# Key block diagonals written by the eviction with a 0/1 column, and a packed layout for the small inputs

## The chip, the cores and the metric
The kernel runs on one core of a Trainium2 chip. The metric is the device time of one execution in microseconds (us); lower is better. The core has a matrix engine (PE), a vector engine (DVE), a scalar engine (ACT), a third elementwise engine (POOL) and a queue engine (SP) that issues nearly all DMAs. The engines run at the same time, each takes its own instructions strictly in order, and they wait for each other through semaphores.

## The reference, cut to what matters
Sixteen independent batch elements of 128 tokens by 256 channels, all float32, go through two blocks:

```python
m = silu(cond) @ w_ada + b_ada           # 9 vectors of 256 per batch element: shift, scale, gate, three times
h = ln(x) * (1 + sc_msa) + sh_msa        # SELF:  16 heads of 16, 128x128 scores per head
x = x + (softmax(q k^T / 4) v @ w_so + b_so) * g_msa
h = ln(x) * (1 + sc_mca) + sh_mca        # CROSS: keys and values from ctx, the 16 largest scores of 128 kept
x = x + (softmax(top16(q k^T / 4)) v @ w_co + b_co) * g_mca
h = ln(x) * (1 + sc_mlp) + sh_mlp        # MLP:   silu(a) * b of 1024 each
x = x + (silu(a) * b @ w_m2 + b_m2) * g_mlp
xq, xkv = ada_ln(x, cond), ada_ln(ctx, cond)   # LAST:  keys and values from the normalised ctx (CTX)
x = x + softmax(q k^T / 4) v @ Wp + bp
```

## The kernel before
Each batch element b runs through five stages: SELF, CTX (keys and values of both cross attentions, made from ctx), CROSS, MLP and LAST. Several batch elements are in flight, each in another stage.

**The order of the work** is fixed ahead of time. Five tables (SP_PLAN, POOL_PLAN, ACT_PLAN, DVE_PLAN, PE_PLAN, lines 52 to 133) give each step an offset, START gives each stage of each b a number, and steps() (L136) sorts by the sum. The numbers are sort keys and no times. A step stands in the order of its engine wherever the sum puts it, and if it has to wait, all that stands behind it on that engine waits too.

**Scores.** The scores of one attention of one b ("scores", L904 to 923) are eight matmuls into s_bank, four PSUM banks that hold all 16 heads. There is one s_bank, so the 48 score steps of the program take turns. Scores of SELF b and CROSS b are two turns or more apart, and the turn goes in the steady part LAST, CROSS, SELF. The next scores can start once the exponentials (and, for CROSS, the first cut of the top-16 search) have read the bank. All other matmul results go through a ring of four PSUM banks, taken in the order of use and given back by their eviction.

Two heads share one score matmul: 32 rows of q hold two heads of 16, and the keys come as a block diagonal, head 0's rows in the left 128 columns with zeros on the right, head 1's rows in the right 128 columns with zeros on the left. Keys are in k_self, k_cross and k_last with 2, 2 and 4 slots for batch elements.

**How the block diagonals are made before.** "qk" (L872) projects q and k of SELF for b into one ring bank. DVE evicts all of it with its bias into qk_t (L687, 128x512). "k2" (L885) does the same for the keys of CROSS and LAST into k2_t (L694, 128x512). POOL has set the block tiles to zero at the start (L465). Then SP, at "place" (L425 to 436), waits for the eviction and issues eight DMAs per tile that copy 16 rows each to their half (L373): eight for SELF, sixteen for CROSS and LAST, 24 for each b. Scores wait for k_placed (L910), and evictions of k2 wait until the DMAs have read k2_t (L692).

**ctx.** It is loaded once as 128 tokens by 256 (L361). "turn" of CTX (L860 to 871) transposes it raw (two matmuls against the identity, L867) and normalised (two more, L870); ACT copies the raw half out (L535).

**Setup before.** cond comes as 16x256, goes through tanh on ACT and two DVE operations, is transposed by PE (L829) and copied. Thirteen bias vectors come by twelve small DMAs (L386) as 60 rows of 128, are transposed by PE (L824) and spread by DVE (L616 to 633). The gates' biases come by four DMAs (L390, L392). "mods" (L842) multiplies silu(cond) with the weights that give scale and shift of a stage, "rows" (L851) gives the gates, which go to DRAM and come back as broadcast loads (L364). The three parts of w_ada come as 768 KB each.

Of the kernel before, what the change touches and what calls it, by code (L numbers as in the profile page):

```python
# [51 lines left out]
SP_PLAN = (
    ("load", "cond", None, 226.752), ("load", "gb", None, 235.686), ("load", "so", None, 248.240),
    ("load", "rows", None, 254.344), ("load", "ada0", None, 263.081), ("place", SELF, SELF, 298.546),
    ("load", "ada2", None, 303.744), ("load", "co", None, 311.157), ("load", "x0", None, 312.291),
    ("load", "ada1", None, 317.622), ("load", "qkv", None, 320.311), ("load", "ctx0", None, 320.321),
    ("load", "x1", None, 330.262), ("load", "bp", None, 331.814), ("place", CROSS, CROSS, 346.351),
    ("load", "ss_kv", None, 358.160), ("load_gates", SELF, SELF, 367.495), ("load", "lkv", None, 369.922),
    ("load_ctx", 0, CTX, 370.194), ("store_rows", MLP, None, 397.858), ("load", "x2", None, 411.296),
    ("load", "kv", None, 422.952), ("first_gates", MLP, None, 424.059), ("store_rows", CROSS, None, 427.406),  # L60
    ("store_rows", SELF, None, 433.778), ("load", "x6", None, 434.351), ("load", "lp", None, 436.552),
    ("first_gates", SELF, None, 444.342), ("load", "ctx1", None, 447.588), ("load_gates", CROSS, CROSS, 449.495),
    ("load", "ss_q", None, 456.751), ("store_y", 0, LAST, 465.795), ("load_gates", MLP, MLP, 468.644),
    ("load", "q", None, 468.660), ("load", "x4", None, 480.238), ("load", "x3", None, 485.938),
    ("load_x", 0, LAST, 488.314), ("load", "lq", None, 493.225), ("first_gates", CROSS, None, 493.235),
    ("load", "m1", None, 510.757), ("load", "x5", None, 529.760), ("load", "m2", None, 531.567),
)
# [10 lines left out]
ACT_PLAN = (
    ("shift", SELF, SELF, -36.227), ("v", 0, SELF, -2.370), ("shift", CTX, CTX, 6.791),
    ("exp", (SELF, 0), SELF, 7.093), ("exp", (SELF, 1), SELF, 8.413), ("exp", (SELF, 2), SELF, 9.622),  # L80
    ("exp", (SELF, 3), SELF, 9.942), ("v2", 0, CTX, 26.683), ("T", (SELF, 0), SELF, 33.733),
    ("T", (SELF, 1), SELF, 34.298), ("T", (SELF, 2), SELF, 34.531), ("T", (SELF, 3), SELF, 36.876),
    ("inv", SELF, SELF, 37.653), ("shift", CROSS, CROSS, 52.002), ("exp", (CROSS, 0), CROSS, 66.004),
    ("exp", (CROSS, 1), CROSS, 73.999), ("exp", (CROSS, 2), CROSS, 74.922), ("exp", (CROSS, 3), CROSS, 78.653),
    ("top_exp", 0, CROSS, 81.146), ("T", (CROSS, 0), CROSS, 81.913), ("T", (CROSS, 1), CROSS, 81.920),
    ("T", (CROSS, 2), CROSS, 82.806), ("T", (CROSS, 3), CROSS, 83.460), ("inv", CROSS, CROSS, 84.882),
    ("shift", MLP, MLP, 91.150), ("tanh", 0, MLP, 97.308), ("tanh", 1, MLP, 98.175), ("half", 0, MLP, 103.625),
    ("half", 1, MLP, 105.370), ("shift", LAST, LAST, 125.349), ("exp", (LAST, 0), LAST, 131.955),
    ("exp", (LAST, 1), LAST, 133.173), ("exp", (LAST, 2), LAST, 133.815), ("exp", (LAST, 3), LAST, 136.413),
    ("T", (LAST, 0), LAST, 139.376), ("T", (LAST, 1), LAST, 142.428), ("T", (LAST, 2), LAST, 145.168),  # L90
    ("T", (LAST, 3), LAST, 146.105), ("inv", LAST, LAST, 150.744),
)
DVE_PLAN = (
    ("stats", SELF, SELF, -62.647), ("aggr", SELF, SELF, -61.830), ("cond", 0, None, -60.987),
    ("stats", CTX, CTX, -25.918), ("qk", 0, SELF, -24.776), ("aggr", CTX, CTX, -22.218),
    ("max", (SELF, 0), SELF, 1.754), ("bias", 0, None, 2.756), ("silu", 0, None, 6.770),
    ("max", (SELF, 1), SELF, 7.259), ("k2", 0, CTX, 15.767), ("inv", SELF, SELF, 20.340), ("o", SELF, SELF, 39.280),
    ("rows", SELF, None, 39.486), ("gate", SELF, SELF, 43.321), ("add", SELF, SELF, 43.495),
    ("stats", CROSS, CROSS, 43.948), ("aggr", CROSS, CROSS, 45.523), ("q", CROSS, CROSS, 61.535),
    ("rows", MLP, None, 63.287), ("mods", SELF, None, 64.135), ("top_a", 0, CROSS, 65.492),  # L100
    ("top_a", 1, CROSS, 65.498), ("cut_a", 0, CROSS, 65.723), ("cut_a", 1, CROSS, 65.845),
    ("top_a", 2, CROSS, 66.141), ("top_b", 0, CROSS, 67.290), ("top_b", 1, CROSS, 67.343),
# [908 lines left out]
```

## Time and profile before

| what | value |
|---|---|
| three runs | 689.52 us median, 685.43 to 690.34 |
| profiled execution | 688.72 us |
| its span | 686.5 us (2.2 us lie outside) |
| mean granted clock of PE over the span | 0.963 |
| PE, DVE, ACT, POOL busy in us | 615.2, 522.9, 496.2, 372.8 |

A busy share tells how long an engine had an instruction in it. PE's matmuls are pipelined, so its busy time is not all work at full rate. Cover each other: what an engine does while another one is the late one costs nothing. The granted clock is in tenths or as a fraction of full speed, 2.4 GHz; half of it is 1.2 GHz.

### The profile page before, as it was taken

The numbers are of one execution on the slowest core, as the hardware profiler recorded it, in microseconds if no ns is written. First come the engines' busy times: TensorE is split into PE (matmuls) and PEld (weight loads), VectorE is DVE, ScalarE is ACT, GpSimd is POOL, SyncE is SP. The second block draws the span as 40 slices with busy tenths as digits, with TensorE's granted clock in tenths as the row PEclk, the third lists the DMA queues.
The fourth block names the chain that finished last, engine by engine and source line by source line (L and its number), as shares of the span: only waits on it lengthen the run. The fifth ranks groups of instructions, "written<-read, shape, count | busy, mean of one in ns | idle before, by whom it ended". The sixth has DMA issues, their size and how long they took to land.

```text
span 686.5 us, 18283 instructions
## 1 busy us (share of the span) xinstructions
PE 615.2 (90%) x5899; PEld 534.3 (78%) x5899; DVE 522.9 (76%) x2201; ACT 496.2 (72%) x1906; POOL 372.8 (54%) x623
## 2 busy tenths in 40 slices
PE   3966787899999999999999999999999999886786
PEld 1755576798989788888889898989897988775564
DVE  3223857889898979798979898898989797968232
ACT  0154464888888787979887887878888878755174
POOL 3223543757575747665756666674747472737220
PEclk9898899999999999999999999999999999999697
DMA  6352261110203020202020202102020201010000
GB/s 210 117 169 74 65 216 25 40 24 17 76 8 88 6 81 14 84 12 79 16 77 19 75 21 66 29 23 73 12 74 5 80 9 45 11 40 1 24 1 16
DMA packets 37740, 36.43 MB, mean 53 GB/s; under 512 B 8115, under 2 KB 29151, under 8 KB 37391
## 3 DMA queue, kind: packets, MB, share of 16 engines
q1 hardware_dynamic: 37647, 35.27, 16.9%
q8 instruction: 48, 0.79, 0.5%
q14 instruction: 45, 0.37, 0.2%
HBM read 26.75 MB, written 2.20 MB: 42 GB/s over the span
## 4 chain that ended last, share of the span: by engine, by line
DVE 42%; PE 25%; ACT 15%; POOL 6%; issue 5%; SPq 4%; DMA 2%; POOLq 0%; DVEq 0%
ACT probs L566 13%; DVE left L724 9%; DVE left L737 9%; DVE top L713 7%; DVE top L731 7%; PE ring L816 6%; PE ring L810 5%; PE s_bank L920 4%; DVE neg_max L705 3%; SPq L373 3%; PE ring L976 3%; DVE mlp L784 2%; POOL left L505 2%; PE ring L933 2%; PE ring L953 2%
## 5 line engine op out<-in xcount | busy, mean ns | idle before, releaser
L566 ACT ACTIVATE probs<-s_bank,neg_max 128x128 f32<-128x128 f32 x512 | 181.1, 411 | 14.0 <-DVE neg_max L705 12.6
L976 PE MATMUL ring<-h_t,w_m 128*128 128x128 f32 x1024 | 126.4, 280 | 5.2 <-DVE k_t L694 3.5
L566 ACT ACTIVATION_READ_ACCUMULATOR probs<-s_bank,neg_max 128x1 f32 x512 | 129.0, 252 | 0.0
L976 PEld LDWEIGHTS ring<-h_t,w_m 128*128 128x128 f32 x1024 | 120.6, 195 | 10.7 <-issue 8.3
L573 ACT ACTIVATE probs_t<-ring 128x512 f32<-128x512 f32 x192 | 110.6, 629 | 23.7 <-PE ring L933 23.1
L563 ACT ACTIVATE probs<-s_bank,neg_max 128x128 f32<-128x128 f32 x256 | 73.7, 399 | 49.3 <-DVE left L724 49.3
L705 DVE TENSOR_REDUCE neg_max<-s_bank 128x8 f32<-128x1024 f32 x64 | 76.1, 1203 | 25.5 <-PE s_bank L920 25.1
L538 ACT ACTIVATE h_t<-ring,mod_all 128x128 f32<-128x128 f32 x160 | 63.2, 482 | 40.9 <-PE ring L870 40.8
L505 POOL TENSOR_TENSOR left<-left,probs 128x512 f32<-128x512 f32 x64 | 83.6, 1306 | 9.8 <-POOL left L501 0.4
L519 POOL TENSOR_TENSOR mlp<-mlp 128x512 f32<-128x512 f32 x32 | 40.8, 1274 | 72.1 <-ACT mlp L595 72.1
L933 PE MATMUL ring<-ident,probs 128*128 128x128 f32 x512 | 71.8, 275 | 6.6 <-ACT probs L566 3.2
L478 POOL TENSOR_SCALAR ln_var<-ln_mv 128x1 f32<-128x1 f32 x80 | 15.4, 193 | 110.0 <-DVE ln_mv L682 108.2
L933 PEld LDWEIGHTS ring<-ident,probs 128*128 128x128 f32 x512 | 59.9, 142 | 11.6 <-ACT probs L566 6.1
L724 DVE MATCH_REPLACE8 left<-top,s_bank 128x128 f32<-128x128 f32 x256 | 68.7, 277 | 0.0
L737 DVE MATCH_REPLACE8 left<-top,left 128x128 f32<-128x128 f32 x256 | 67.5, 273 | 0.0
L984 PE MATMUL ring<-w_m,mlp 128*128 128x256 f32 x256 | 58.2, 380 | 2.6 <-POOL mlp L519 2.5
L713 DVE MAX8 top<-s_bank 128x8 f32<-128x128 f32 x256 | 54.8, 279 | 2.5 <-PE s_bank L920 2.4
L984 PEld LDWEIGHTS ring<-w_m,mlp 128*128 128x128 f32 x256 | 47.4, 190 | 9.1 <-POOL mlp L519 3.3
L595 ACT ACTIVATE mlp<-ring,bias_cols 128x128 f32<-128x128 f32 x128 | 36.8, 381 | 24.2 <-PE ring L976 23.9
L731 DVE MAX8 top<-left 128x8 f32<-128x128 f32 x256 | 53.7, 276 | 0.6
L501 POOL TENSOR_SCALAR left<-left 128x512 f32<-128x512 f32 x64 | 39.6, 618 | 25.8 <-DVE left L737 22.9
L497 POOL TENSOR_TENSOR x_res<-x_res,gates 128x256 f32<-128x256 f32 x48 | 34.9, 728 | 33.9 <-DMA gates<-rows_dram 33.7
(127 smaller groups left out, 1270.1 us busy)
## 6 DMA issues: line engine op xcount, KB each, us to landing
gates<-rows_dram SPq DMA_DIRECT2D x48, 256.0 KB, 4.0
x_res<-in_x SPq DMA_DIRECT2D x16, 128.0 KB, 3.8
ctx_in<-in_ctx SPq DMA_DIRECT2D x16, 128.0 KB, 3.9
k_self<-qk_t SPq DMA_DIRECT2D x128, 16.0 KB, 2.3
k_cross<-k_t SPq DMA_DIRECT2D x128, 16.0 KB, 1.9
k_last<-k_t SPq DMA_DIRECT2D x128, 16.0 KB, 1.9
w_m<-in_L_xcond_w_m SPq DMA_DIRECT2D x1, 2048.0 KB, 7.7
out_y<-x_res SPq DMA_DIRECT2D x16, 128.0 KB, 1.7
```

Source lines behind the costliest of these rows:

```text
L505: nc.gpsimd.tensor_tensor(left[:, u], left[:, u], probs[:, CROSS, u], ALU.add).then_inc(masked, 1)
L563: e = nc.scalar.activation(probs[:, k, u, j], s_bank[:, u, P * j:P * j + P], ACT.Exp, bias=neg_max[:, k, n:n + 1])
L566: e = nc.scalar.activation(probs[:, k, u, j], s_bank[:, u, P * j:P * j + P], ACT.Exp, bias=neg_max[:, k, n:n + 1], accum_out=row_sum[:, k, ...
L573: nc.scalar.activation(dst, bank("T", which, b)[:], ACT.Relu if k == CROSS else ACT.Copy).then_inc(pt_ready, 1)
L705: nc.vector.tensor_reduce(neg_max[:, k, 8 * half:8 * half + 8], s_bank[:, 2 * half:2 * half + 2].rearrange("p u (j t) -> p (u j) t", t=P), ...
L713: e = nc.vector.max(top16[:, 4 * u + j, 0:8], s_bank[:, u, P * j:P * j + P])
L724: e = nc.vector.match_replace(left[:, u, j], top16[:, 4 * u + j, 0:8], s_bank[:, u, P * j:P * j + P], GONE)
L731: e = nc.vector.max(top16[:, 4 * u + j, 8:16], left[:, u, j])
L737: e = nc.vector.match_replace(left[:, u, j], top16[:, 4 * u + j, 8:16], left[:, u, j], GONE)
L933: e = nc.tensor.transpose(d[:, P * j:P * j + P], src[:, j], ident[:])
L976: e = nc.tensor.matmul(d[:, P * j:P * j + P], w_m1[:, c, at:at + P], h_t[:, MLP, c], start=(c == 0), stop=(c == CK - 1))
L984: e = nc.tensor.matmul(d[:, 0:C], glu[:, j // 4, j % 4], w_m2[:, j], start=(j == 0), stop=(j == HB - 1))
```

## The change
The key blocks are written by the eviction itself. A column `halves` (128x2) holds 0 or 1 per row: column 0 is 1 on rows of head 0 of each pair, column 1 on rows of head 1. POOL sets up its source once (three small instructions) and DVE makes the two columns (two small instructions). key_blocks() then issues for each 128 channels one scalar_tensor_tensor from PSUM: (k + bias) * halves, 256 elements wide, the PSUM operand read twice. That is two instructions for SELF and four for CROSS and LAST per b. q of SELF has its own eviction, 256 wide. All `place` steps, the k_placed semaphores and the zeroing of the key tiles go. "k2" now waits for the scores that read the slot it writes.

The host lays out inputs differently (reordering only): weights with 128 partitions outermost and contiguous rows, cond transposed as 128x32, all bias columns as 128x54, the gates' biases in one array, and a second copy of ctx that is already transposed (ctx_t). So the transposes of ctx (L867), its copy out (L535), and the transposes of cond and biases go. w_ada's parts come split in scale/shift (512 KB) and gate (256 KB), w_qkv in q/k (512 KB) and v (256 KB). A second load per b brings ctx_t (128 KB). The next ctx_in load waits for "norm" instead of "turn". The five tables and START are written anew, so the order of steps changes in many places; the order of the 48 score steps among themselves is the same as before.

```diff
-    SELF: (123.491, 159.058, 201.581, 240.471, 280.069, 319.014, 357.908, 396.794,
+    SELF: (189.635, 227.561, 267.927, 306.804, 346.245, 385.716, 425.902, 465.078,
 ...
-    ("load", "rows", None, 254.344), ("load", "ada0", None, 263.081), ("place", SELF, SELF, 298.546),
+    ("load", "cond", None, -835.363), ("load", "ada0", None, -819.429), ("load", "vecs", None, -732.506),
 ...
-            def place(kind, b, src):
-                s = b % SLOTS[kind]
-                if b >= SLOTS[kind]:
-                    sp.wait_ge(scores_done, PE_N["scores", kind, b - SLOTS[kind]])
-                for g in range(8):
-                    rows_g = slice(16 * g, 16 * g + 16)
-                    sp.dma_start(k_blocks[kind][rows_g, s, :, g % 2, :], src[rows_g]).then_inc(k_placed[kind, s], 16)
 ...
                 if name == "load_ctx" and b + 2 < B:
-                    sp.wait_ge(turned, PE_N["turn", CTX, b])
+                    sp.wait_ge(normed, POOL_N["norm", CTX, b])
                     load_ctx(b + 2)
+                if name == "load_ctx_t" and b + 2 < B:
+                    sp.wait_ge(k2_done, b + 1)
+                    sp.wait_ge(v2_done, b + 1)
+                    load_ctx_t(b + 2)
 ...
-                    if k == CTX:
-                        nc.scalar.copy(ctx_t[:].rearrange("p c t -> p (c t)"), src[:, 0:C])
-                        at = C
 ...
+            def key_blocks(k, b, d, at):
+                for c in range(CK):
+                    src = d[:, C + at + P * c:C + at + P * c + P]
+                    e = nc.vector.scalar_tensor_tensor(
+                        out=k_blocks[k][:, b % SLOTS[k], c], in0=src.unsqueeze(1).broadcast_to([P, 2, P]),
+                        scalar=bias_cols[:, NK + 2 * k + c:NK + 2 * k + c + 1],
+                        in1=halves[:].unsqueeze(2).broadcast_to([P, 2, P]), op0=ALU.add, op1=ALU.mult)
+                return e
 ...
                 if name == "qk":
-                    if b >= 2:
-                        dve.wait_ge(k_placed[SELF, b % 2], 16 * 8 * (b // 2))
+                    if b >= SLOTS[SELF]:
+                        dve.wait_ge(scores_done, PE_N["scores", SELF, b - SLOTS[SELF]])
                     dve.wait_ge(qk_done, b + 1)
-                    nc.vector.tensor_tensor(qk_t[:, b % 2], blocks(bank("qk", 0, b), 4), cols(NQ_SELF, 4),
-                                            ALU.add).then_inc(qk_ready, 1)
+                    d = bank("qk", 0, b)
+                    nc.vector.tensor_tensor(q_t[:, SELF, b % 2], blocks(d, CK), cols(NQ + 2 * SELF, CK), ALU.add)
+                    key_blocks(SELF, b, d, 0).then_inc(qk_ready, 1)
                 if name == "k2":
-                    if b:
-                        for k in (CROSS, LAST):
-                            dve.wait_ge(k_placed[k, (b - 1) % SLOTS[k]], 16 * 8 * ((b - 1) // SLOTS[k] + 1))
+                    for k in (CROSS, LAST):
+                        if b >= SLOTS[k]:
+                            dve.wait_ge(scores_done, PE_N["scores", k, b - SLOTS[k]])
                     dve.wait_ge(k2_done, b + 1)
-                    nc.vector.tensor_tensor(k2_t[:], blocks(bank("k2", 0, b), 4), cols(NK_CTX, 4),
-                                            ALU.add).then_inc(k2_ready, 1)
+                    d = bank("k2", 0, b)
+                    key_blocks(CROSS, b, d, -C)
+                    key_blocks(LAST, b, d, 0).then_inc(k2_ready, 1)
```

**How the order moves.** The rows below give the line, the instruction and, in brackets, the semaphores it waits for. First PE from the program's start, before. probs_t holds w_ada's part for SELF, mlp those for MLP and CROSS, probs the weights of scale and shift of CTX (later of LAST):

```order
L829 MATMUL ring<-ident,probs_t 128x16 [waits setup_dve,consts_ready]
...
L824 MATMUL ring<-ident,probs_t 128x60 [waits rows_loaded]
L816 MATMUL ring<-probs_t,silu_t 16x256 [waits bias_ready,silu_ready,w_loaded_so,w_loaded_ada0]
...
L816 MATMUL ring<-w_so,bv_rows 16x256 x2
L816 MATMUL ring<-mlp,silu_t 16x256 [waits silu_ready,bias_ready,w_loaded_ada2]
...
L842 MATMUL ring<-silu_t,probs_t 128x16 [waits silu_ready,w_loaded_ada0]
...
L842 MATMUL ring<-silu_t,mlp 128x16 [waits bias_evicted,w_loaded_ada2,silu_ready]
...
L842 MATMUL ring<-silu_t,mlp 128x16 [waits rows_evicted,w_loaded_ada1,silu_ready]
```

The same stretch of PE in the changed kernel:

```order
L812 MATMUL ring<-silu_t,probs_t 128x16 [waits w_loaded_ada0,silu_ready,consts_ready]
...
L796 MATMUL ring<-probs_t,silu_t 16x256 [waits bias_ready,silu_ready,w_loaded_so,w_loaded_ada0g]
...
L796 MATMUL ring<-w_so,bv_rows 16x256 x2
L835 MATMUL ring<-ident,x_norm 128x128 [waits normed]
...
L812 MATMUL ring<-silu_t,probs 128x16 [waits w_loaded_ss_kv,silu_ready]
...
L790 MATMUL ring<-h_t,w_qkv 128x128 [waits h_ready,mods_ready,w_scaled,w_loaded_qk]
...
L796 MATMUL ring<-w_qkv,h_t 128x256 [waits rows_evicted,h_ready,w_loaded_v]
```

The transposes of cond and biases are gone, "mods" of SELF is first, and "mods" of MLP and CROSS and "rows" of MLP have moved behind the first "qk".

SP around the first two placements, before:

```order
L420 DMA rows_dram<-left 16x512 [waits rows_ready]
L358 DMA x_res<-in_x 128x256
L373 DMA k_self<-qk_t 16x2x128 [waits zeroed,qk_ready]
L373 DMA k_self<-qk_t 16x2x128 x7
L355 DMA w_kv<-in_L_xcond_w_kv 128x2x512
L364 DMA gates<-rows_dram 128x512 [waits rows_stored3]
...
L361 DMA ctx_in<-in_ctx 128x256
L373 DMA k_self<-qk_t 16x2x128 [waits qk_ready]
...
L355 DMA w_q<-in_L_xcond_w_q 128x2x256
L373 DMA k_cross<-k_t 16x2x128 [waits zeroed,k2_ready]
```

SP from its first waiting instruction on in the changed kernel:

```order
L399 DMA rows_dram<-left 16x512 [waits rows_ready]
L358 DMA x_res<-in_x 128x256
L355 DMA l_q<-in_w_lq 128x512
...
L355 DMA mlp<-in_w_ada 128x2x512
L364 DMA ctx_t<-in_ctx_t 128x256
...
L367 DMA gates<-rows_dram 128x512 [waits rows_stored0]
...
L355 DMA w_q<-in_w_q 128x512
L364 DMA ctx_t<-in_ctx_t 128x256 [waits v2_done,k2_done]
...
L361 DMA ctx_in<-in_ctx 128x256 [waits normed]
L355 DMA w_m<-in_w_m 128x4096
```

No placement stands between the loads any more, and 21 DMAs are issued ahead of the first wait.

DVE in one turn of the steady part, from the eviction of q and k of SELF to the top-16 search, before:

```order
L687 TENSOR_TENSOR qk_t<-ring,bias_cols 128x512
L677 BN_STATS ln_stats<-x_res 128x6
L705 TENSOR_REDUCE neg_max<-s_bank 128x8
...
L677 BN_STATS ln_stats<-ctx_in 128x6
...
L779 TENSOR_TENSOR mlp<-ring,bias_cols 128x512
...
L694 TENSOR_TENSOR k_t<-ring,bias_cols 128x512
...
L699 TENSOR_TENSOR q_t<-ring,bias_cols 128x256
L748 RECIPROCAL inv_row<-row_sum 128x4x2x2
L784 SCALAR_TENSOR_TENSOR mlp<-mlp 128x512 x2
L713 MAX top<-s_bank 128x8 x8
```

The same in the changed kernel:

```order
L666 TENSOR_TENSOR q_t<-ring,bias_cols 128x256
L587 SCALAR_TENSOR_TENSOR k_self<-ring,bias_cols,halves 128x256 x2
L685 TENSOR_REDUCE neg_max<-s_bank 128x8 x2
L655 BN_STATS ln_stats<-ctx_in 128x6
...
L587 SCALAR_TENSOR_TENSOR k_cross<-ring,bias_cols,halves 128x256 x2
L587 SCALAR_TENSOR_TENSOR k_last<-ring,bias_cols,halves 128x256 x2
L759 TENSOR_TENSOR mlp<-ring,bias_cols 128x512 x2
L728 RECIPROCAL inv_row<-row_sum 128x4x2x2
L679 TENSOR_TENSOR q_t<-ring,bias_cols 128x256
L764 SCALAR_TENSOR_TENSOR mlp<-mlp 128x512 x2
L693 MAX top<-s_bank 128x8 x8
```

The keys' evictions stand at the same places, are longer, and k2's now stands ahead of both linear evictions of the MLP (the step "lin").

## Rows read from the trace of the kernel before

**Rows 1.** Windows: length, busy (instructions) by engine, clock, DMA share, GB/s.

```profile
0.00:20.00 20.00, 8.82 (x39) 4.97 (x39) 8.04 (x20) 1.70 (x2) 8.23 (x15) 1.00 0.63 216
20.00:40.00 20.00, 15.94 (x98) 12.37 (x98) 4.22 (x11) 2.86 (x8) 2.89 (x8) 0.78 0.30 104
172.59:208.18 35.59, 35.40 (x364) 31.75 (x363) 31.57 (x137) 30.74 (x120) 22.71 (x39) 1.00 0.16 46
244.63:282.00 37.37, 35.59 (x364) 31.78 (x363) 31.40 (x137) 31.03 (x120) 23.19 (x39) 1.00 0.15 46
354.20:390.55 36.35, 35.49 (x364) 31.81 (x363) 31.98 (x137) 30.75 (x120) 22.54 (x39) 1.00 0.16 48
```

**Rows 2.** Timeline of PE, score steps: start, length, instruction, [idle before <-releaser].

```profile
37.57 1.67 PE L920 MATMUL s_bank<-k_self,qk_t 32*128 32x256 f32 x16 [4.06 <-DMA k_self<-qk_t]
51.86 2.09 PE L920 MATMUL s_bank<-k_self,qk_t 32*128 32x256 f32 x16 [1.01 <-issue]
68.55 2.09 PE L920 MATMUL s_bank<-k_cross,q_t 32*128 32x256 f32 x16 [4.84 <-DVE q_t L699]
108.95 1.51 PE L920 MATMUL s_bank<-k_cross,q_t 32*128 32x256 f32 x16
137.02 1.15 PE L920 MATMUL s_bank<-k_last,q_t 32*128 32x256 f32 x16 [0.16 <-ACT probs L566]
571.41 1.15 PE L920 MATMUL s_bank<-k_last,q_t 32*128 32x256 f32 x16 [1.07 <-ACT probs L566]
```

**Rows 3.** Timeline of PE in the first 35 us.

```profile
11.90 1.89 PE L816 MATMUL ring<-probs_t,silu_t 128*16 128x256 f32 x4 [3.19 <-DMA probs_t<-in_L_xcond_w_ada]
17.13 2.16 PE L842 MATMUL ring<-silu_t,probs_t 128*128 128x16 f32 x16
19.14 5.31 PE L842 MATMUL ring<-silu_t,mlp 128*128 128x16 f32 x32
28.15 2.05 PE L810 MATMUL ring<-h_t,w_qkv 128*128 128x128 f32 x16
32.91 0.38 PE L867 MATMUL ring<-ident,ctx_in 128*128 128x128 f32 x2
```

**Rows 4.** DMA issues: queue, count, size of one, median us to landing.

```profile
probs_t<-in_L_xcond_w_ada SPq DMA_DIRECT2D x1, 768.0 KB, 4.5
probs<-in_L_xcond_Wss_kv SPq DMA_DIRECT2D x1, 512.0 KB, 10.6
k_self<-qk_t SPq DMA_DIRECT2D x128, 16.0 KB, 2.3
```

**Rows 5.** Timeline of SP, issues of the placements and one load.

```profile
45.45 5.05 SPq L373 DMA_DIRECT2D k_self<-qk_t  x8
53.06 5.46 SPq L373 DMA_DIRECT2D k_cross<-k_t  x8
64.03 0.83 SPq L358 DMA_DIRECT2D x_res<-in_x  x2
97.08 5.18 SPq L373 DMA_DIRECT2D k_self<-qk_t  x8
```

**Rows 6.** Timeline of DVE.

```profile
66.90 0.43 DVE L677 BATCH_NORM_STATS2 ln_stats<-x_res 128x6 f32<-128x256 f32 x1 [4.89 <-DMA x_res<-in_x]
104.61 0.43 DVE L677 BATCH_NORM_STATS2 ln_stats<-ctx_in 128x6 f32<-128x256 f32 x1 [6.94 <-DMA ctx_in<-in_ctx]
353.65 0.42 DVE L699 TENSOR_TENSOR q_t<-ring,bias_cols 128x256 f32<-128x256 f32 x1 [0.81 <-PE ring L810]
353.99 0.68 DVE L687 TENSOR_TENSOR qk_t<-ring,bias_cols 128x512 f32<-128x512 f32 x1
354.59 0.42 DVE L677 BATCH_NORM_STATS2 ln_stats<-x_res 128x6 f32<-128x256 f32 x1
361.11 0.69 DVE L779 TENSOR_TENSOR mlp<-ring,bias_cols 128x512 f32<-128x512 f32 x1 [0.43 <-PE ring L976]
362.91 1.49 DVE L784 SCALAR_TENSOR_TENSOR mlp<-mlp 128x512 f32<-128x512 f32 x2 [0.26 <-ACT mlp L587]
```

More of the change, by code:

```diff
@@ L57 @@
[L57 to L61, printed above, removed]
@@ L77 @@
+    ("scale", LAST, None, 324.348),
 )
 ACT_PLAN = (
[L79 to L83, printed above, removed]
@@ L92 @@
 )
 DVE_PLAN = (
[L94 to L102, printed above, removed]
-    ("cut_b", 0, CROSS, 67.535), ("cut_a", 2, CROSS, 68.629), ("mods", MLP, None, 68.704),
-    ("cut_b", 1, CROSS, 68.737), ("top_b", 2, CROSS, 68.910), ("top_a", 3, CROSS, 69.295),
@@ new lines @@
+    ("silu_mul", 0, MLP, 110.337), ("silu_mul", 1, MLP, 110.928), ("gate", MLP, MLP, 121.630),
+    ("add", MLP, MLP, 123.598), ("stats", LAST, LAST, 125.556), ("aggr", LAST, LAST, 126.459),
+    ("q", LAST, LAST, 136.983), ("max", (LAST, 0), LAST, 140.295), ("max", (LAST, 1), LAST, 140.863),
+    ("inv", LAST, LAST, 148.846), ("o", LAST, LAST, 161.791), ("mods", CTX, None, 165.205),
+    ("rows", SELF, None, 166.782), ("add", LAST, LAST, 168.553), ("rows", CROSS, None, 183.314),
+    ("rows", MLP, None, 200.055), ("mods", MLP, None, 245.611), ("mods", CROSS, None, 246.801),
@@ L115 @@
+    ("mods", LAST, None, 260.307), ("last", 0, None, 310.092),
 )
 PE_PLAN = (
-    ("silu", 0, None, -313.698), ("bias", 0, None, -226.294), ("rows", SELF, None, -212.684),
-    ("turn", SELF, SELF, -43.063), ("qk", 0, SELF, -30.856), ("rows", MLP, None, -13.780), ("v", 0, SELF, -8.038),
-    ("scores", SELF, SELF, -2.255), ("turn", CTX, CTX, 4.022), ("k2", 0, CTX, 11.855), ("v2", 0, CTX, 20.806),
-    ("mods", SELF, None, 24.708), ("T", (SELF, 0), SELF, 27.657), ("T", (SELF, 1), SELF, 28.424),
@@ L133 @@
+    ("scores", LAST, LAST, 131.855), ("T", (LAST, 0), LAST, 138.341), ("T", (LAST, 1), LAST, 139.915),
+    ("T", (LAST, 2), LAST, 143.901), ("T", (LAST, 3), LAST, 146.327), ("inv", LAST, LAST, 147.533),
+    ("sums", LAST, LAST, 152.412), ("out", LAST, LAST, 161.343), ("mods", CTX, None, 162.231),
+    ("rows", CROSS, None, 181.589), ("rows", MLP, None, 199.664), ("mods", CROSS, None, 238.898),
+    ("mods", MLP, None, 240.469), ("mods", LAST, None, 241.796), ("last", 0, None, 305.966),
 )
@@ L141, in steps @@
         yield name, which, b
-BANKED = {"bias", "silu", "mods", "rows", "last", "turn", "qk", "v", "k2", "v2", "q", "T", "inv", "sums", "out", "up", "down"}
+BANKED = {"mods", "rows", "last", "turn", "qk", "v", "k2", "v2", "q", "T", "inv", "sums", "out", "up", "down"}
 USE = {}
```

353 lines of the change are left out of this document (174 added, 179 removed).

## The prediction, made before the result was known
> **What bounds the kernel now.** I read the page's busy times first (PE 615 of 686.5 us, DVE 523), then the start times of the score steps, because they cut the program into a fill, a steady part and a tail. The first scores of SELF start at 37.57, the first of LAST at 137.02 and the thirteenth of LAST at 571.41 [rows 2]. So the fill is 137.0 us, twelve turns take 434.4 us, which is 36.2 each, and the tail is 686.5 - 571.4 = 115.1.
>
> Then the windows. In a steady turn of 35.59 to 37.37 us PE is busy 35.4 to 35.6 at full clock, DVE 31.4 to 32.0, ACT 30.7 to 31.0 [rows 1]. PE has almost no gap, so the steady part is PE's own work plus 0.2 to 1.8 us per turn. The fill is another matter: in the first 20 us PE is busy 8.8, and from 20 to 40 its clock is 0.78, a mix of 2.4 and 1.2 GHz [rows 1]. There the timeline shows what it waits for. The first scores wait 4.06 us for the placement of k_self [rows 2]. Eight placement issues hold SP for 5.0 to 5.5 us and the last lands 2.3 us after its issue [rows 4, 5]; in that time no load behind them is issued. Two such loads come late: x_res is issued at 64.03, behind 16 placements, and DVE stands 4.89 us for it, which keeps q of CROSS from PE's first CROSS scores for 4.84 us; and ctx_in, behind the placements from 97.08 to 102.26, holds DVE for 6.94 us in front of k2's eviction [rows 2, 5, 6].
>
> **The change, part by part**
>
> *Until the first scores.* Before, PE starts its main work at 11.90, when 768 KB of w_ada have come: a load of 4.5 us that was issued after 18 others [rows 3, 4]. In the changed kernel 512 KB of it are SP's second DMA. It is issued near 1.2 and, by that row, lands by 5.2. From there I add what stands in PE's order up to the first scores: "mods" of SELF 2.2, "rows" of SELF 1.9 + 1.9, a turn and the shift on ACT 1.8, "mods" of CTX 2.2, "qk" 2.05, "v" 1.7, "rows" of CROSS 1.9 + 1.9, two turns 0.7, all at the durations of the slow clock [rows 3]. That is 18.3, so the first scores come at 23.5, which is **-14.1**. Of this, 5.31 (the two "mods" for MLP and CROSS) and 1.9 ("rows" of MLP) are only moved behind the scores [rows 3] and come back below. The loads could be later than I take them: 512 KB for CTX took 10.6 us from issue to landing in a full queue [rows 4], and issued near 5 that would be 15.6 instead of the 12.8 at which PE asks for it. Bounds: -8 (weights late by 3, the moved work at once in the way) to -17 (no wait and a warm clock).
>
> The Trainium skill (DMA: Bandwidth & Descriptors, Specifications) wants at least 512 bytes per transfer for full rate, and cond (128 bytes a row) and the bias columns (216 bytes a row) now lie under that, where before they lay at or above it. By that page these two loads are poor. They are 16 and 27 KB, and the rows here do not show such a load. Nothing in the sum rests on this.
>
> *First to second scores of SELF, 14.3 us before.* The second placement is issued from 45.45 to 50.50, and the scores start at 51.86 [rows 2, 5]. It goes; "rows" of MLP, a longer "qk" and "v2" now lie in the same stretch. **-1**, bounds -4 to +2.
>
> *Second scores of SELF to the first of CROSS, 16.7 us.* The 4.84 us go, since the x loads are now ahead of any late wait on SP; 5.31 at a cold clock, about half at a warm one, for the moved "mods" come in, partly where PE would wait for SELF's residual anyway. **-1.5**, bounds -5 to +2.
>
> *First to second scores of CROSS, 40.4 us.* DVE's 6.94 go with the placements ahead of ctx_in. PE had other work for a part of it, so I take **-4.9**, the same size as the other stall; bounds -3 to -7. From there to the first LAST scores (28.1 us) I take nothing. The fill gives -14.1 - 1 - 1.5 - 4.9 = **-21.5**; LAST's first scores come at 115.5. Bounds together -11 to -29.
>
> *DVE in the steady part.* Its instructions overlap, so I take start-to-start times: 0.34 for 256 wide (353.65 to 353.99) and 0.60 for 512 (353.99 to 354.59) [rows 6]. The trace has no scalar_tensor_tensor from PSUM; the one from SBUF of 512 takes 1.49 for two, much like the other forms, so I take 0.34 for 256. SELF's keys: 3 x 0.34 instead of 0.60, +0.42. k2: 4 x 0.34 instead of 0.60, +0.76. Together **+1.18 per batch element**, DVE 31.5 + 1.2 = 32.7 of 36. It stays under PE. What hides it: SELF's eviction stands before LAST's maxima, which wait for PE's scores; k2's stands between these maxima and silu_mul, while ACT makes LAST's exponentials. "lin" of the second half starts at 361.11 only because PE is that late (0.43 idle), and silu_mul again waits 0.26 for ACT at 362.91 [rows 6]. With k2's 0.76 and the second stats ahead of "lin", I count on lin starting at most as late as PE's second "up" allows. I charge 0; if that cover were gone, all of it would be 1.18 x 12 = +14 over the steady part.
>
> The Trainium skill (VectorE: DVE Perf Modes, the section on the TRN2 errata) puts an operation from PSUM at 120 cycles plus its elements, at 0.96 GHz: 0.39 us for 256 wide and 0.66 for 512. By it the change adds 7 x 0.39 - 2 x 0.66 = 1.4 us per element, against the 1.18 of the rows; the rows decide.
>
> *PE.* Two raw transposes of ctx per element go, 0.22 us of work (two take 0.38 with overlap, 0.11 start to start) [rows 3]. They stand just ahead of LAST's scores, in the stretch that is PE's own. -0.22 per turn.
>
> *ACT* loses one copy per element, *SP* 24 issues and gains one. Neither was late in the steady part, except where SP's placements delayed ctx_in: the turn of 37.37 against 35.59 is the size of it [rows 1]. On the other hand the new order lets POOL's last mask wait at other places. I take **-0.2 per turn, -2.4** over twelve. Bounds: -0.8 (all turns as short as the best one less 0.22, 35.4) to +1.18, so -10 to +14.
>
> *Tail.* After the last k2 nothing of the change is in it but the order; 0, bounds -2 to +2.
>
> **Sum:** 688.7 (profiled execution) - 21.5 - 2.4 = 664.8. The median of the runs is 0.8 above that execution, so 665.
>
> **The rivals**
>
> *Weights or gates come late in the fill.* For: the first 20 us already move 216 GB/s at 0.63 of the DMA engines' time [rows 1], and the changed kernel asks for ss_kv, qk, v and co within 18 us. Against: 21 DMAs go out without a wait. The fill then gives -11, and the time is 689.5 - 11 - 2.4 = 676.
>
> *DVE's extra work is not covered.* For: DVE is at 88% of a turn and the top-16 search is one long DVE stretch on which SELF's scores wait. Against: the new evictions do not stand in that stretch. +14 on the steady part: 689.5 - 21.5 + 14 = 682 at the full 1.18, 679 with PE's 0.22 and the ctx waits taken off.
>
> *The steady part drops to PE's floor.* With no placement, no late ctx_in and fewer transposes, turns of 35.4: 689.5 - 21.5 - 10 = 658.
>
> *Slower: k2's eviction delays the MLP.* It now stands ahead of both "lin". If (k + bias) * halves, with its PSUM operand read twice, took much longer than a plain eviction, "lin" would be late, then tanh on ACT, silu_mul, and with them the start of the top-16 search, which sets SELF's scores and so the turn. To eat 23.9 us over about 14 turns it needs 1.7 per turn on the path. The cover there is about 0.7 (0.43 + 0.26 [rows 6]), and the six instructions take the place of 1.20 - 0.34 = 0.86 (two plain evictions less q's own), so together they would have to cost 0.86 + 0.7 + 1.7 = 3.26, which is 0.54 us each from start to start. At 0.60, the pace of a 512 wide one [rows 6], the turn grows by 6 x 0.60 - 0.86 - 0.7 = 2.0 and the time is 689.5 - 21.5 + 14 x 2.0 = 696. Against: the output has 256 elements per instruction, and 256 wide ones take 0.42 here whatever their kind.
>
> **How the numbers follow.** Forecast (650 to 672) 0.52; late weights (676) 0.17; uncovered DVE work (679 to 682) 0.12; PE's floor (658 and under) 0.14; slower by k2 0.05. The predicted time is **665**. The range takes in the floor with a better fill, 689.5 - 29 - 8 = 652, and the uncovered DVE work, 682. About 1% (7 us) is what a measurement of this kernel tells from no change, its three runs spread over 0.7%. Faster by over 1% (under 682.6): 0.91; within 1%: 0.05 (uncovered work together with late weights); slower: 0.04.
>
> **What would show it.** In the trace after: "mods" of SELF on PE by 6, first scores of SELF at 21 to 27, first of LAST at 110 to 122; key_blocks instructions of about 0.42 us with 0.34 between starts; DVE busy 32 to 33.5 per turn; turns of 35.5 to 36.5. It would be wrong if the fill still ended past 128, if turns were 37 and more with DVE named as what PE waits for, or if PE waited for weights between 5 and 20 us for more than 5 us in sum.

## The result, and the profile after

The changed kernel takes 683.43 us (median of 20 runs, 680.40 to 689.52) against 689.41 for the kernel before (20 runs, 685.43 to 691.55). The ratio is 0.9933, with a 95% interval of 0.9912 to 0.9954. That is 0.7% faster where 665 us was forecast, outside the range of 652 to 682. The profiled execution took 683.1 us with a span of 681.4 (before: 688.72 and 686.5).

The score steps cut its time into the same three parts as before. The start times on PE, to be held against [rows 2]:

```profile
22.95 1.15 PE L887 MATMUL s_bank<-k_self,q_t 32*128 32x256 f32 x16
33.81 1.15 PE L887 MATMUL s_bank<-k_self,q_t 32*128 32x256 f32 x16
50.07 1.15 PE L887 MATMUL s_bank<-k_cross,q_t 32*128 32x256 f32 x16
84.01 1.15 PE L887 MATMUL s_bank<-k_cross,q_t 32*128 32x256 f32 x16
113.38 1.15 PE L887 MATMUL s_bank<-k_last,q_t 32*128 32x256 f32 x16
566.78 1.15 PE L887 MATMUL s_bank<-k_last,q_t 32*128 32x256 f32 x16 [0.59 <-ACT probs L542]
```

The fill ends at 113.38 instead of 137.02: -23.6 us. The twelve turns behind it take 566.78 - 113.38 = 453.4 us, 37.78 each, where they took 434.4, 36.20 each: **+19.0**. The tail is 114.6 against 115.1. So the fill gained what was forecast, and four fifths of it were lost again, evenly over the steady turns. The windows of four turns, in the columns of [rows 1], show it:

```profile
151.33:188.07 36.74, 36.12 (x361) 31.36 (x360) 34.06 (x142) 30.59 (x119) 22.75 (x39) 1.00 0.13 37
188.07:225.88 37.81, 36.23 (x362) 31.41 (x361) 34.52 (x142) 30.59 (x119) 22.59 (x39) 1.00 0.14 37
264.03:301.98 37.95, 36.23 (x362) 31.41 (x361) 34.91 (x142) 30.45 (x119) 22.76 (x38) 1.00 0.08 28
301.98:339.68 37.70, 36.23 (x362) 31.42 (x361) 34.50 (x142) 30.58 (x119) 23.16 (x39) 1.00 0.11 35
```

The clock is full in all of them, so it is no part of the loss. DVE is busy about 3 us more per turn, where seven evictions of 256 (six of keys, one of q) instead of two plain ones of 512 should give 1.2 to 1.5. The surplus is found in the chain of waits, the view that says which piece of work each next one waited for. One turn of the kernel before, from scores to scores (start, length, what; the middle of the top-16 search left out):

```profile
327.01 1.29 DVE mlp L784 x2
328.30 1.60 DVE top L713 x8
329.90 0.06 DVE neg_max L721
...
331.03 0.07 DVE neg_max L721
...
335.54 0.07 DVE neg_max L721
...
340.32 0.07 DVE neg_max L721
...
343.62 0.63 POOL left L501
```

The same stretch in the changed kernel:

```profile
272.75 2.01 DVE mlp L764 x2
274.76 1.60 DVE top L693 x8
276.36 0.06 DVE neg_max L701
...
279.05 0.06 DVE neg_max L701
...
281.22 1.13 DVE neg_max L701
...
287.83 0.31 DVE neg_max L701
...
291.37 0.63 POOL left L479
```

From the end of silu_mul (the line "mlp") to the mask of GpSimd (POOL) on which the next transposes wait, it is 16.61 us after (274.76 to 291.37) and 15.32 before (328.30 to 343.62). All 1.29 of it is in one tiny operation, neg_max<-top: a tensor_scalar that negates four numbers per partition, in the step cut_a. silu_mul itself takes 2.01 instead of 1.29. From scores to scores these two turns last 35.90 and 37.95 us, and the 1.29 and the 0.72 of silu_mul are 2.01 of the 2.05 between them. The sums over the execution (busy time, mean ns of one), before first:

```profile
L784 DVE SCALAR_TENSOR_TENSOR mlp<-mlp 128x512 f32<-128x512 f32 x32 | 21.6, 709 | 3.6 <-ACT mlp L587 3.6
L721 DVE TENSOR_SCALAR neg_max<-top 128x4 f32<-128x4 f32 x64 | 12.5, 196 | 0.0
```

```profile
L764 DVE SCALAR_TENSOR_TENSOR mlp<-mlp 128x512 f32<-128x512 f32 x32 | 27.5, 893 | 3.9 <-ACT mlp L563 3.9
L701 DVE TENSOR_SCALAR neg_max<-top 128x4 f32<-128x4 f32 x64 | 29.1, 455 | 0.0
```

And this is what stands beside them on POOL in that turn of the changed kernel:

```profile
272.75 2.01 DVE L764 SCALAR_TENSOR_TENSOR mlp<-mlp 128x512 f32<-128x512 f32 x2 [0.27 <-ACT mlp L563]
273.05 1.16 POOL L475 TENSOR_TENSOR x_res<-x_res,b_last 128x256 f32<-128x256 f32 x1
274.17 1.86 POOL L475 TENSOR_TENSOR x_res<-x_res,gates 128x256 f32<-128x256 f32 x2
...
279.83 2.50 POOL L497 TENSOR_TENSOR mlp<-mlp 128x512 f32<-128x512 f32 x2 [3.46 <-ACT mlp L571]
281.14 1.21 DVE L701 TENSOR_SCALAR neg_max<-top 128x4 f32<-128x4 f32 x1
```

The two glu multiplies of POOL run from 279.83 to 282.33. neg_max starts at 281.14 and ends at 282.35, with the second of them. The last neg_max of the search, the 0.31 of the chain, ends with another POOL operation, a product for the masks that runs to 288.12:

```profile
286.85 1.27 POOL L483 TENSOR_TENSOR left<-left,probs 128x512 f32<-128x512 f32 x1
...
287.76 0.39 DVE L701 TENSOR_SCALAR neg_max<-top 128x4 f32<-128x4 f32 x1
```

In the kernel before, the two multiplies start 2.22 us apart in the turn of the chain above and 2.68 in the next one, and the same neg_max lands behind the second. In this next turn it meets a residual add that runs to 371.92, and takes 0.39:

```profile
367.28 1.28 POOL L519 TENSOR_TENSOR mlp<-mlp 128x512 f32<-128x512 f32 x1 [4.02 <-ACT mlp L595]
...
369.96 1.28 POOL L519 TENSOR_TENSOR mlp<-mlp 128x512 f32<-128x512 f32 x1 [1.40 <-ACT mlp L595]
...
371.20 0.72 POOL L497 TENSOR_TENSOR x_res<-x_res,gates 128x256 f32<-128x256 f32 x1
...
371.57 0.39 DVE L721 TENSOR_SCALAR neg_max<-top 128x4 f32<-128x4 f32 x1
```

Over the whole trace of the changed kernel it is the same: 34 of the 64 neg_max start while a POOL operation has more than 0.1 us to go, and each of them ends 0.02 to 0.03 us after that operation. The other 30 take 0.139 to 0.151 us. Of the time above 0.15 us, 13.8 us stand beside the glu multiplies, 4.1 beside the mask products, 1.9 beside adds and copies.

The tables of the change did this: ACT's two "half" steps now follow each other directly, so POOL's glu multiplies do too, and the third cut_a stands one place earlier in DVE's top-16 order (seven steps ahead of it, before eight). The second of these is tested below; ACT's part was not put back by itself.

**Theory A:** DVE operations of some forms (neg_max, a tensor_scalar from SBUF to SBUF, and silu_mul with two inputs in SBUF) wait until the POOL operation in progress has ended. The new order brought neg_max (and silu_mul) into such collisions; the key evictions cost nothing. **Rival B:** the key evictions are the cost, since they lengthen DVE's work. **Rival C:** anything on DVE at that place is held up.

### The profile page after: what moved, and what is told of

Read it like the earlier page. It is cut to its first block, busy times and chain, and to the rows that moved or that the text cites. A ratio compares the mean times of both kernels' runs of the same rounds, so it can differ in the third digit from the quotient of the medians.

```text
span 681.4 us, 17865 instructions
## 1 busy us (share of the span) xinstructions
PE 617.0 (91%) x5864; PEld 529.8 (78%) x5864; DVE 562.6 (83%) x2276; ACT 493.0 (72%) x1891; POOL 367.8 (54%) x623
## 4 chain that ended last, share of the span: by engine, by line
DVE 44%; PE 31%; ACT 16%; POOL 5%; issue 2%; DMA 1%; SPq 1%; DVEq 0%; POOLq 0%; ACTq 0%
ACT probs L542 13%; DVE left L704 9%; DVE left L717 9%; PE ring L796 8%; PE ring L790 7%; DVE top L693 7%; DVE top L711 7%; DVE mlp L764 4%; DVE neg_max L701 3%; PE ring L920 3%; PE s_bank L887 3%; POOL left L483 3%; PE ring L900 3%; DVE neg_max L685 3%; PE ring L943 2%
## 5 line engine op out<-in xcount | busy, mean ns | idle before, releaser
L549 ACT ACTIVATE probs_t<-ring 128x512 f32<-128x512 f32 x192 | 112.2, 629 | 40.4 <-PE ring L900 40.2
L943 PE MATMUL ring<-h_t,w_m 128*128 128x128 f32 x1024 | 121.2, 277 | 1.8 <-ACT h_t L514 1.8
L943 PEld LDWEIGHTS ring<-h_t,w_m 128*128 128x128 f32 x1024 | 118.3, 194 | 2.3 <-ACT h_t L514 2.3
L514 ACT ACTIVATE h_t<-ring,mod_all 128x128 f32<-128x128 f32 x160 | 66.2, 509 | 38.9 <-PE ring L835 38.9
L951 PE MATMUL ring<-w_m,mlp 128*128 128x256 f32 x256 | 60.9, 392 | 2.3 <-POOL mlp L497 2.1
L900 PE MATMUL ring<-ident,left 128*128 128x128 f32 x256 | 38.2, 283 | 20.3 <-POOL left L483 14.9
L900 PEld LDWEIGHTS ring<-ident,left 128*128 128x128 f32 x256 | 28.0, 142 | 32.1 <-POOL left L483 18.9
```

What stands on the lines that cost most here:

```text
L549: nc.scalar.activation(dst, bank("T", which, b)[:], ACT.Relu if k == CROSS else ACT.Copy).then_inc(pt_ready, 1)
L900: e = nc.tensor.transpose(d[:, P * j:P * j + P], src[:, j], ident[:])
L943: e = nc.tensor.matmul(d[:, P * j:P * j + P], w_m1[:, c, at:at + P], h_t[:, MLP, c], start=(c == 0), stop=(c == CK - 1))
L951: e = nc.tensor.matmul(d[:, 0:C], glu[:, j // 4, j % 4], w_m2[:, j], start=(j == 0), stop=(j == HB - 1))
```

## The experiments

**neg_reduce.** One operation takes another form, in the changed kernel:

```
- nc.vector.tensor_scalar(neg_max[:, CROSS, 4*u:4*u+4].unsqueeze(2), top16[:, 4*u:4*u+4, 0:1], -1.0, None, ALU.mult)
+ nc.vector.tensor_reduce(neg_max[:, CROSS, 4*u:4*u+4], top16[:, 4*u:4*u+4, 0:1], AX.X, ALU.max, negate=True)
```

> The changed kernel, with the one small step neg_max<-top (128x4, two per quarter of the CROSS scores... four per batch, a tensor_scalar from SBUF to SBUF) written as a tensor_reduce with negate of the same four numbers. Theory A (that tensor_scalar is held up by GpSimd's two glu multiplies: 1.13 and 0.31 us of it stand in the chain of one turn, where the kernel before has 0.06 to 0.07 each): the op costs 0.05 to 0.15 us every time, a steady turn falls from 37.8 to 36.3 to 36.8 us, the whole to 662 to 670 us. Rival B (the four more key evictions on VectorE are what made the turn longer): the op gets shorter but the turn stays at 37.4 or more and the whole within 3 us of 683. Rival C (any op that reads SBUF there is held up): the reduce takes 1.2 us in the same place, no change.

Measured: 665.3 us, ratio 0.9647 (0.9610 to 0.9683), twelve turns of 36.45. Same numbers, same place, same neighbours on POOL, and the operation is free of the wait (36 of the 64 start with a POOL operation in progress, and none takes over 0.201 us):

```profile
L701 DVE TENSOR_REDUCE neg_max<-top 128x4 f32<-128x4 f32 x64 | 10.2, 159 | 0.0
```

In the same turn as above (now 36.65 us long, 37.95 before the edit) its four pieces of the chain are 0.06, 0.06, 0.07 and 0.06, and the search takes 15.29 us. All of the search's extra time is gone; silu_mul still takes 2.02. B and C fall. The same kernel once more:

> The first substitution once more, unchanged, beside the kernel before on the same chip, because its runs spread from 663 to 668 us: 662 to 669 us, turn 36.3 to 36.6.

Measured: 667.81 us, ratio 0.9685 (0.9647 to 0.9723), turns of 36.45 again. Of the 5.1 us between the two profiled executions (spans 661.0 and 666.1), 2.7 lie in the fill and 2.4 in the tail.

**before_neg_reduce.** The same edit in the kernel before.

> The same substitution in the kernel before. Theory A: there the op was mostly clear of the glu multiplies (mean 0.196 us of 64, 12.5 us in all), so at most 4 to 6 us come off, 683 to 688 us. Rival: if the reduce is a gain by itself, whatever stands beside it, then 10 us or more come off here as well (under 679).

Measured: 684.83 us, ratio 0.9924 (0.9897 to 0.9951), 36.03 a turn instead of 36.20. The form of the operation is worth 5 us where it rarely collides and 16 to 18, by the medians, where it collides in every turn.

**before_keys.** The kernel before, its tables and loads kept, with the key evictions alone:

```
- nc.vector.tensor_tensor(k2_t[:], blocks(bank("k2", 0, b), 4), cols(NK_CTX, 4), ALU.add)
+ key_blocks(CROSS, b, d, -C, NK_CTX)
+ key_blocks(LAST, b, d, 0, NK_CTX + CK)
- place(CROSS, b, k2_t[:, 0:CK]); place(LAST, b, k2_t[:, CK:2 * CK])      (and the same for SELF)
```

> The kernel before with the key blocks written by the eviction (no placements, no zeroing of key blocks, the odd/even columns set up), everything else, loads and the tables with the order of the work, as before. Theory A (the new order of the top-16 steps and of the glu steps costs the 1.6 us a turn, not the evictions): steady turn 36.0 to 36.6 us, and with the placements gone from the fill the whole at 670 to 680 us. Rival B (the evictions on VectorE cost it): turn at 37.2 or more, 685 to 700 us.

Measured: 671.72 us, ratio 0.9738 (0.9709 to 0.9767); fill 119.60, turns of 36.27. So the change from placements to evictions costs 0.07 us a turn and takes 17.4 us out of the fill, and this part of the change alone beats the whole of it by 11.7 us.

**neg_reduce_keys_twice.** neg_reduce with LAST's two key evictions written a second time, to a spare tile.

> The changed kernel with the tensor_reduce, and the two key evictions of LAST (2 x 0.40 to 0.48 us) written a second time, into a spare tile, in each of the 16 k2 steps: 0.8 to 0.9 us more of VectorE a turn. Theory A (the k2 evictions stand where VectorE waits anyway): 0 to 0.15 us a turn, 665 to 668 us in all. Rival B (they delay lin, tanh, silu_mul and so the top-16 steps, all of it uncovered): 0.85 x 16 = 13.6 us more, 677 to 680 us. Half covered: 671 to 673.

Measured: 663.96 us, ratio 0.9643 (0.9611 to 0.9676), turns of 36.51, +0.06. Even 0.8 us more of such work on DVE is covered.

**top_order.** The changed kernel with DVE's sixteen top-16 steps in the order of the kernel before (only due times in the table exchanged).

> The changed kernel with the 16 top-16 steps of VectorE put back into the order that they had in the kernel before (the second cut ahead of the third search, the third cut after the second late search), nothing else. Theory A: the third cut's neg_max op comes one step (about 0.5 to 0.9 us) later and lands mostly behind the two glu multiplies, so its wait falls from 1.2 us to 0.3 or less, and the turn to 36.8 to 37.3, the whole to 668 to 677 us. If the op runs into another GpSimd op instead, less comes off: 677 to 683 us. Rival B: 683, as the change.

Measured: 675.15 us, ratio 0.9788 (0.9756 to 0.9819), turns of 36.90; neg_max costs 17.4 us in all, mean 271 ns. The order of these sixteen steps alone was 0.9 of the 1.6 us a turn.

**glu_split.** Each glu multiply of POOL cut into four of 128x128; neg_max is a tensor_scalar as in the change.

```
+ for j in range(4):
+     nc.gpsimd.tensor_tensor(glu[:, half, j], tanh_a[:, half, j], glu[:, half, j], ALU.mult)
```

> The changed kernel with each of the two glu multiplies of GpSimd (128x512, 1.25 us) cut into four of 128x128; the tensor_scalar neg_max<-top stays. Theory A (a tensor_scalar of VectorE that reads and writes SBUF waits until the GpSimd operation that holds the port has ended, whatever its own size): its wait falls from up to 1.2 us to at most the length of a piece (0.3 to 0.5 us), the turn from 37.8 to 37.0 to 37.5 us, the whole to 671 to 680 us; GpSimd's extra instructions may give 0.3 of it back. Rival (it waits until GpSimd has no work left at all, or for something else than the multiplies): 1.2 us stays, 683 or more.

Measured: 673.62 us, ratio 0.9784 (0.9744 to 0.9823), turns of 37.21. Now neg_max waits for a piece, not for 1.2 us, although POOL works on for 1.6 us behind it. In 15 of the 16 batch elements it takes 0.415 to 0.429:

```profile
277.20 3.36 POOL L498 TENSOR_TENSOR mlp<-mlp 128x128 f32<-128x128 f32 x8 [3.47 <-ACT mlp L573]
278.50 0.42 DVE L703 TENSOR_SCALAR neg_max<-top 128x4 f32<-128x4 f32 x1
```

So the wait is set by the one POOL operation in progress. Beside the mask products, which were not cut, neg_max still takes up to 0.87 us, and the mean of all 64 is 336 ns.

**neg_reduce_top_order.** Both edits.

> Both at once: neg_max<-top as a tensor_reduce, and the top-16 steps in the order of the kernel before. Theory A: with the op immune, the order has nothing left to dodge, so the time is that of the first substitution, 665.3, within 2 us (663.5 to 667.5), turn 36.3 to 36.6. Rival: the order is worth something by itself (masks of GpSimd and transposes reached earlier): 2 to 6 us less, 659 to 663, or more.

Measured: turns of 36.44, as with the reduce alone (36.45), and a profiled execution of 662.63 us. The median is 669.8 (ratio 0.9728, 0.9691 to 0.9765), 2.3 above the expectation; its four other runs lie at 669 to 670. Their mean granted clock was 0.959 to 0.962, against 0.974 in the profiled one. That goes with the longer time, but no trace shows where those 7 us lie. On the steady turns theory A holds: with the operation immune, the order is worth nothing.

**neg_reduce_skip_late and neg_reduce_skip_gap.** These went for silu_mul. In the first, POOL's residual adds of LAST and SELF are due behind the glu multiplies; in the second, behind the spread and ahead of them.

> The changed kernel with the tensor_reduce, and GpSimd's residual adds (skip) of LAST and SELF moved from ahead of the glu multiplies to behind them, so that they no longer lie beside VectorE's silu_mul (two inputs in SBUF, 2.02 us for two in a turn where the kernel before takes 1.29 to 1.4). Theory A: silu_mul falls to 1.3 to 1.5 us, 0.4 to 0.7 us a turn, the whole to 655 to 661 us. Rival 1: the adds then delay the masks of the top-16 cut and with them the transposes, so it comes out at 665 or more. Rival 2: PE bounds the turn by then (36.2 busy of 36.4) and nothing is gained, 664 to 666.

> The changed kernel with the tensor_reduce, and GpSimd's residual adds of LAST and SELF moved into the 3.5 us in which GpSimd waits for ScalarE's half steps, ahead of the glu multiplies and behind the spread, so that only the MLP add may lie beside silu_mul, and the masks are not behind them. Theory A (silu_mul's two SBUF inputs are held up by the adds): silu_mul 1.3 to 1.5 us for two instead of 2.02, turn 35.9 to 36.2, the whole 657 to 662 us. Rival: the glu multiplies are late and the masks with them, or silu_mul is held up by the norm of GpSimd that takes the adds' place: no gain, 664 to 668.

Measured: 670.93 us (ratio 0.9764, 0.9701 to 0.9827), turns of 37.02; and 664.81 us (0.9663, 0.9622 to 0.9705), turns of 36.44. Both missed. The first made POOL's masks late: the transposes of the masked scores waited 16.2 us for them in all, 6.9 with neg_reduce_top_order. And silu_mul did not get shorter in either (867 and 922 ns), because POOL, which works down its list without a break, just ran its next operations there. In the second:

```profile
266.91 2.01 DVE L764 SCALAR_TENSOR_TENSOR mlp<-mlp 128x512 f32<-128x512 f32 x2 [0.26 <-ACT mlp L563]
267.22 1.16 POOL L475 TENSOR_TENSOR x_res<-x_res,gates 128x256 f32<-128x256 f32 x1
268.32 0.86 POOL L490 COPY inv_wide<-inv_row 128x256 f32<-128x256 f32 x1
```

The add that takes 0.73 us elsewhere takes 1.16 and the copy 0.86 instead of 0.40. Both engines lose here. Neither order tried kept POOL away; a wait did.

**neg_reduce_skip_hold.** The second of these, and the add of MLP waits for silu_mul:

```
+ if which == MLP:
+     pool.wait_ge(silu_done, DVE_N["silu_mul", 1, b])
```

> The kernel of the run before (tensor_reduce, the adds of LAST and SELF in GpSimd's gap), and GpSimd's add of MLP waits for the second silu_mul too, so that neither it nor the spread behind it lies beside silu_mul. Theory A (any GpSimd operation from and to SBUF that has started holds up silu_mul, there an add of 1.16 us and a copy of 0.86 us in the 2.01 us): silu_mul takes 1.29 to 1.35 us for two in every turn, 0.4 to 0.7 us less a turn on average where it was 2.01 (1.84 on average), so 0.3 to 0.6 a turn, 655 to 662 us. Rival: what comes off silu_mul is waited for elsewhere (GpSimd's glu multiplies and masks start later, or PE), and the turn stays at 36.3 or more, 663 to 668.

Measured: **655.65 us, ratio 0.9523 (0.9494 to 0.9553)**, turns of 35.99, the fastest of all. This kernel differs from neg_reduce_skip_gap by the wait alone, so the wait is worth 0.45 us a turn. The adds are back at their own length. silu_mul takes 1.29 to 1.31 us for two in six of the twelve steady turns and 1.47 to 1.49 in the other six, so the expected 1.29 to 1.35 in every turn was only half met; in the turn of 263.99 the norm's last POOL operation (263.77 to 264.32) is still in progress when it starts. POOL's wait costs nothing, since POOL idled later for ACT's "half" anyway (3.44 us before glu, now 2.46):

```profile
L766 DVE SCALAR_TENSOR_TENSOR mlp<-mlp 128x512 f32<-128x512 f32 x32 | 22.0, 722 | 3.9 <-ACT mlp L565 3.9
L477 POOL TENSOR_TENSOR x_res<-x_res,gates 128x256 f32<-128x256 f32 x48 | 34.8, 726 | 38.7 <-DVE mlp L766 38.7
```

## Why the prediction was wrong, and where it was right

*Until the first scores, -14.1.* Measured -14.6 (37.57 to 22.95). "mods" of SELF starts at 5.12, forecast 5.2, and weights are waited for only once more, 1.47 us, for ss_kv. That the rest came out is partly luck. All steps were taken "at the durations of the slow clock", and "mods" of SELF (3.57 us against 2.2) and "qk" (3.66 against 2.05) took longer, by 2.7 from start to start, while "v" (1.05 against 1.7) and "rows" of CROSS (1.04 + 1.03 against 1.9 + 1.9) made up for 2.7. The granted clock was 0.51 from 16.1 to 19.5 us, where "qk" stands, and 0.99 from 19.5 to 23.0. It was 1.00 from 5.1 to 8.6, so why "mods" took 3.57 is not shown.

```profile
5.12 3.57 PE L812 MATMUL ring<-silu_t,probs_t 128*128 128x16 f32 x16 [5.12 <-DMA probs_t<-in_w_ada]
...
14.30 1.93 PE L812 MATMUL ring<-silu_t,probs 128*128 128x16 f32 x16 [1.47 <-DMA probs<-in_w_ss_kv]
```

*The other terms of the fill.* First to second SELF scores -3.4 (forecast -1), on to CROSS -0.4 (-1.5), to the second CROSS -6.5 (-4.9), to LAST +1.3 (0). Together -23.6 against -21.5, and the parts are off by more than the sum. before_keys divides it: the placements alone give 17.4; what is left, 6.2, goes to loads, layout and order by difference, not by a run of its own. These 6.2 are two larger numbers: the first SELF scores come another 11.2 us earlier than in before_keys (34.15 to 22.95), and the stretch from the second SELF scores to the first CROSS scores, into which "mods" of MLP and CROSS moved, gets 5.0 longer (11.31 to 16.26). The rival of late weights fell.

*The key evictions, +1.18 per element, all covered.* Right, and shown two ways (before_keys +0.07 a turn, keys twice +0.06). The size: four of them take 0.39 to 0.40 us each from start to start, against the 0.34 taken from [rows 6].

```profile
268.50 0.88 DVE L587 SCALAR_TENSOR_TENSOR k_cross<-ring,bias_cols,halves 128x256 f32<-128x256 f32 x2
269.29 0.87 DVE L587 SCALAR_TENSOR_TENSOR k_last<-ring,bias_cols,halves 128x256 f32<-128x256 f32 x2
270.07 0.68 DVE L759 TENSOR_TENSOR mlp<-ring,bias_cols 128x512 f32<-128x512 f32 x1
```

The Trainium skill (VectorE: DVE Perf Modes, the section on the TRN2 errata) gave an estimate of 0.39 for this width, and the trace agrees with its 0.39 to 0.40; here the page was nearer than the row that I preferred. The wrong size did no harm, since the work was covered. The signs set out for "uncovered DVE work" (turns over 37, DVE at 34.9) did appear, with another cause: those signs could not tell more work from longer waits inside the same work.

*The steady part, -0.2 per turn, -2.4.* **This is the step that failed: +1.6 per turn, +19.0.** Its bounds, -10 to +14, did not hold it either. It was made from the work that the change adds and takes away, and only in one sentence ("the new order lets POOL's last mask wait at other places") from the order. What was missing is the pairing: which POOL operation lies beside which DVE operation. 1.33 us a turn is neg_max (37.78 to 36.45 with the reduce), and 0.46 silu_mul and its neighbours (36.45 to 35.99 with the hold); the kernel before had a small share of the first (0.17 a turn by before_neg_reduce). Against the kernel before, neg_max is so +1.16 a turn, and silu_mul, 1.83 us for two on average over the twelve turns against 1.34, is +0.49; together 1.65, and the two transposes less take 0.2 off by the estimate of the prediction. With both treated the changed kernel is at 35.99, and the kernel before with the reduce at 36.03, so all else in the new order and the evictions costs a steady turn nothing on balance.

The Trainium skill (SBUF — State Buffer, "Who interferes with whom") says how this works: a DVE tensor_scalar from SBUF that can run in a mode with two ports, and any DVE operation with two SBUF inputs against a POOL operation that reads SBUF, takes a port pair shared with POOL as an exclusive lock, and the later one waits in full. The runs agree: 1.21 us for an operation that takes 0.14 to 0.15 alone, 0.42 with the POOL operations cut in four, and 0.159 on average as tensor_reduce, which the same section excepts. The traces show the wait, not the port. I had read the trace for price and cover only; neg_max's longest 525 ns in the kernel before (median 156) was there to be seen as such a wait.

*PE's floor.* The prediction held that "the steady part is PE's own work plus 0.2 to 1.8 us", since PE was busy 35.4 to 35.6 of a turn. But PE's busy time is not a fixed sum of work: it was 36.23 us in a turn of 37.95, 36.13 in 36.65 (neg_reduce) and 35.83 in 36.00 (neg_reduce_skip_hold), with 361 to 363 instructions each time. At 36.13 of 36.65 PE looked like the bound, and the next 0.46 us still came off the turn.

```profile
262.00:298.00 36.00, 35.83 (x362) 31.25 (x361) 33.03 (x142) 30.59 (x120) 20.86 (x37) 1.00 0.12 38
```

The chain of the turn shown above has PE in it for 9.4 us (the last 8.3 before LAST's scores, and these scores); 16.6 are DVE's top-16 search, and when neg_reduce took 1.06 and 0.25 us out of it, 1.30 came off the turn (37.95 to 36.65). A chain of one steady turn, read before predicting, would have put the search at the centre and asked what can disturb it.

*The sum.* 664.8 and the 0.8 of the median are 665.6, which the prediction gives as 665; nothing hangs on it.

*The tail, 0.* Measured -0.5. The rival in which k2's eviction delays "lin" fell with the cover of the key evictions.

## What to carry to other kernels

Before you add or move work in a schedule by tables, list for the stretch that sets the turn which DVE operations wait for GpSimd (here a tensor_scalar from SBUF to SBUF and a scalar_tensor_tensor with two SBUF inputs) and what GpSimd runs beside them: here a new order cost 1.3 us a turn through an operation of 0.15 us. In the trace such a wait is not idle time but part of the operation's own length, so look for operations whose longest instance is far above the median (here 1219 ns against 358). The cheapest cure here was a form that does not wait (a tensor_reduce with negate); the long operation was protected by a wait on GpSimd's side, where two changes of GpSimd's order had failed. An engine that is busy 98% of a turn is not by that shown to be its bound; look at the chain of one turn.

## What the runs showed of the hardware

- A tensor_scalar on four numbers a partition took 0.14 to 0.15 us alone and 1.22 at most; each of the 34 longer ones ended 0.02 to 0.03 us after a GpSimd operation did; as a tensor_reduce of the same numbers its mean was 0.159 us beside the same neighbours.
- The wait goes both ways. Small GpSimd operations of the norm, 0.19 and 0.55 us alone, took 0.74 and 1.00 beside silu_mul, whose two halves started within 0.01 us of the first and 0.1 us ahead of the second, and silu_mul kept its 1.29 us for two (neg_reduce_skip_gap):

```profile
303.55 0.74 POOL L458 TENSOR_SCALAR ln_neg<-ln_mv 128x1 f32<-128x1 f32 x1
303.55 1.29 DVE L764 SCALAR_TENSOR_TENSOR mlp<-mlp 128x512 f32<-128x512 f32 x2 [0.27 <-ACT mlp L563]
304.26 1.00 POOL L460 TENSOR_TENSOR ln_rstd<-ln_var,minus_half 128x1 f32<-128x1 f32 x1
```

- Long operations on both sides take turns. In the changed kernel's turn above, silu_mul's first half runs from 272.75 to 273.63, the add from 273.05 to 274.21, the second half from 273.55 to 274.76 and the next add from 274.17 to 275.34: each ends 0.55 to 0.59 us after the one before it.
- Two executions of one kernel can take the same 437.4 us for twelve steady turns and differ by 5.1 us in fill and tail; over the whole tail the granted clock was 0.92 in the one and 0.88 in the other.
